# Filling a weight ring only where its expert changes, and asking for rows elsewhere in SyncE's order

## The reference

```python
logits = xn @ router_w                       # 8 experts
topv, topi = jax.lax.top_k(softmax(logits), 2)
topv = topv / sum(topv)
for e in range(8):                           # F = 1024
    gate, up = split(xn @ gate_up_w[e])
    out += comb[:, e] * ((silu(clip(gate, -10, 10)) * up) @ down_w[e])
out += swiglu(xn, shared_gate_up_w, shared_down_w)
```

## Time and profile before

| | |
|---|---|
| median of 3 executions | 1149.23 us (1145.25 to 1150.15) |
| profiled execution, its own time | 1156.33 us |
| its span | 1154.6 us |
| TensorE busy | 1041.0 us (90%) |
| VectorE busy | 800.8 us (69%) |
| DMA, mean | 214 GB/s, 246.72 MB |
| transfers into `single_ring`, issued | 144 in this record, of 768 KB |

### The profile page before, as it was taken

How to read it: one execution, slowest core, us unless ns; L and a number is a source line. 1 busy time by engine, 2 the same in 40 slices (tenths; PEclk the granted TensorE clock), 3 DMA queues, 4 the chain that set the end, 5 groups by cost and what they waited for, 6 DMA issues and landing times.

```text
span 1154.6 us, 22702 instructions
## 1 busy us (share of the span) xinstructions
PE 1041.0 (90%) x7042; PEld 917.3 (79%) x7042; DVE 800.8 (69%) x2051; ACT 623.7 (54%) x1269; POOL 287.1 (25%) x302
## 2 busy tenths in 40 slices
PE   4889999999988998899999999999998699998940
PEld 2666777677666655899999999999998699998940
DVE  5996899897879767566666666666665366665645
ACT  6768868777775364354544544344444244443415
POOL 1133032743252445021212112121121112111125
PEclk9999999999999999899999999999999999999975
DMA  8664766874675588872837264893939945398249
GB/s 305 210 219 168 261 204 223 299 248 146 220 237 188 200 287 300 283 270 65 283 76 235 39 209 128 301 359 76 374 91 330 352 118 164 100 351 263 57 94 216
DMA packets 130715, 246.72 MB, mean 214 GB/s; under 512 B 10848, under 2 KB 76128, under 8 KB 130656
## 3 DMA queue, kind: packets, MB, share of 16 engines
q1 hardware_dynamic: 115248, 226.08, 56.2%
q0 software_dynamic: 15408, 19.93, 9.6%
HBM read 357.61 MB, written 85.50 MB: 384 GB/s over the span
## 4 chain that ended last, share of the span: by engine, by line
PE 68%; DMA 8%; DVE 7%; SPq 7%; issue 4%; ACT 3%; POOL 2%; another core or an unknown queue 1%; DVEq 0%; ACTq 0%; POOLq 0%
PE bank L477 12%; PE bank L1432 8%; PE bank L1434 8%; PE bank L1433 8%; PE bank L1477 4%; PE bank L1479 4%; PE bank L1478 4%; PE bank L471 4%; PE bank L472 4%; PE bank L473 4%; DMA w_both<-w_split 3%; SPq L1302 2%; SPq L1303 1%; PE bank L1448 1%; PE bank L1450 1%
## 5 line engine op out<-in xcount | busy, mean ns | idle before, releaser
L1614 DVE TENSOR_SCALAR cv<-bank 128x256 f32<-128x256 f32 x284 | 120.3, 424 | 182.9 <-PE bank L1434 148.5
L1381 POOL DMA_INDIRECT acc_scratch<-cv,ids x71 | 111.1, 1564 | 541.9 <-DVE cv L1577 518.5
L1544 ACT ACTIVATE cv<-cv 128x256 f32<-128x256 f32 x284 | 118.4, 417 | 210.5 <-DVE cv L1614 207.3
L1432 PE MATMUL bank<-h_hi,w_both 128*128 128x256 f32 x744 | 209.8, 282 | 18.1 <-DMA w_both<-w_split 15.4
L1433 PE MATMUL bank<-h_hi,w_both 128*128 128x256 f32 x744 | 207.3, 279 | 0.0
L1434 PE MATMUL bank<-h_hi,w_both 128*128 128x256 f32 x744 | 207.3, 279 | 0.0
L1432 PEld LDWEIGHTS bank<-h_hi,w_both 128*128 128x128 f32 x744 | 141.0, 190 | 22.0 <-issue 10.5
L1530 ACT ACTIVATE h_lo<-cv 128x256 fp32r<-128x256 f32 x248 | 103.1, 416 | 88.3 <-DVE cv L1617 87.3
L1617 DVE TENSOR_TENSOR cv<-bank,cv 128x256 f32<-128x256 f32 x284 | 120.2, 423 | 41.0 <-ACT cv L1544 37.2
L1434 PEld LDWEIGHTS bank<-h_hi,w_both 128*128 128x128 f32 x744 | 140.9, 189 | 0.0
L1433 PEld LDWEIGHTS bank<-h_hi,w_both 128*128 128x128 f32 x744 | 140.9, 189 | 0.0
(11 more groups left out here) (268 smaller groups left out, 2653.8 us busy)
## 6 DMA issues: line engine op xcount, KB each, us to landing
single_ring<-w_split SPq DMA_DIRECT2D x144, 768.0 KB
w_both<-w_split SPq DMA_DIRECT2D x180, 512.0 KB
w_both<-w_split SPq DMA_DIRECT2D x180, 256.0 KB
e_raw<-w_e SPq DMA_DIRECT2D x64, 384.0 KB
w_split<-e_high SPq DMA_DIRECT2D x64, 384.0 KB
w_split<-e_raw SPq DMA_DIRECT2D x64, 384.0 KB
xs_hi<-w_split SPq DMA_DIRECT2D x30, 512.0 KB
xs_lo<-w_split SPq DMA_DIRECT2D x30, 512.0 KB
```

Source lines behind the costliest of these rows:

```text
L1432: nc.tensor.matmul(out, gu_hi[f][:, cols], xg_hi[:, par, c, :], start=c == 0, stop=False)
L1614: nc.vector.tensor_scalar(half, gate_ps, CLIP, -CLIP, ALU.min, ALU.max).then_inc(clipped, 1)
```

## The change

The second ring is filled only for a single slot whose expert differs from the last single slot's. The plan computes `fresh` for that, multiplies the old flag (`steady`) by it, and writes two tables of nine flags behind each other into `group_change`: fill in the turn n % 4 = 2, and fill in the turn n % 4 = 3. That is five more small VectorE instructions in steps 6 and 7 of slot 0. The ring's eight chunks become three tensors of 5, 2 and 1 places, each filled by one transfer, issued behind chunks 0, 1 and 2. The row request moves from behind chunk 1 to behind chunk 0, and in the turns behind a single slot to behind chunk 7. The rows of slot 2 are asked for ahead of the waits for `ends_cleared` and the scatters.

```diff
-H_AT, XNT_AT, FULL_AT = 146080, 162496, 219456
+H_AT, XNT_AT, FULL_AT = 146336, 162752, 219712
...
+        steady, fresh = [decay[:, 1, (9 + i) * 48:(9 + i) * 48 + NS] for i in range(2)]
+        single_ring = [nc.alloc_sbuf_tensor_at(f"single_ring{at}", [P, places, 2 * CW], F32R, offset=at)
+                       for at, places in ((XNT_AT, 5), (H_AT, 2), (FULL_AT, 1))]
...
             store_shared(2 * B - 1)
+            sp.wait_ge(plan_ready, 1)
+            third_rows()
             sp.wait_ge(ends_cleared, 16 * (E + 2))
             for half in range(2):
                 sp.wait_ge(scattered[half], B * 16 * HT * K)
-            sp.wait_ge(plan_ready, 1)
             other_groups()
...
-            nc.vector.tensor_tensor(group_change[:, NP:SLOTS], thirds[:, :, 2], thirds[:, :, 1], ALU.is_equal)
+            nc.vector.tensor_tensor(steady[:, :], thirds[:, :, 2], thirds[:, :, 1], ALU.is_equal)
...
+                    nc.vector.memset(fresh[:, 0:1], 1.0)
+                    planned(nc.vector.tensor_tensor(fresh[:, 1:NS], code[:, 1:NS], code[:, 0:NS - 1], ALU.not_equal))
...
+                    planned(nc.vector.tensor_tensor(steady[:, :], steady[:, :], fresh[:, :], ALU.mult))
+                    nc.vector.tensor_copy(group_change[:, NP:SLOTS], steady[:, :])
+                    nc.vector.tensor_tensor(group_change[:, SLOTS:SLOTS + NS], fresh[:, :], steady[:, :], ALU.subtract)
...
-        def load_single(f, e, wanted):
-            sp.dma_start(w_single[f][:, :].bitcast(F32), w_s[e, f, :, :], cond=wanted).then_inc(single_loaded, 16)
+        def load_singles(part, e, wanted):
+            first = sum(v.shape[1] for v in w_single[0:part])
+            to = w_single[part].bitcast(F32)
+            sp.dma_start(to, w_s[e, first:first + to.shape[1], :, :].rearrange("f p c -> p f c"), cond=wanted).then_inc(single_loaded, 16)
...
-                flag = to_come if n % BODY == 2 else table_at(i, n - 1)
+                flag = to_come + (0 if n % BODY == 2 else NS)
...
                 load_chunk(f, e, new)
-                if f == 1:
+                if f == (FC - 1 if single(n - 1) else 0):
                     next_rows(i, n)
-                if loads_single:
+                if loads_single and f < len(w_single):
                     if f == 0 and n > BODY:
                         sp.wait_ge(down_done, before(i, n - n % BODY, steps_at) + FC // 2 + FC)
-                    load_single(f, e_single, wanted)
+                    load_singles(f, e_single, wanted)
...
-            next_rows(0, 1)
             free(sp, "x1")
...
-                pe.wait_ge(single_loaded, before(i, n, ones_at) * (32 * FC) + 32 * FC)
+                pe.wait_ge(single_loaded, before(i, n, ones_at) * (32 * len(w_single)) + 32 * len(w_single))
...
-        group_change = sb("group_change", [P, SLOTS], I32)
+        group_change = sb("group_change", [P, SLOTS + NS], I32)
...
+        sb("apart", [P, 3 * LT * 2])
```

More of the change, by code:

```diff
@@ L144, in mixer @@
         unused, expert_f, passed_f, row_f, starred = [decay[:, 1, (4 + i) * 48:(4 + i) * 48 + NP] for i in range(5)]
-        singles_at = [XNT_AT + k * 8 * CW for k in range(5)] + [H_AT + k * 8 * CW for k in range(2)] + [FULL_AT]
-        single_ring = [nc.alloc_sbuf_tensor_at(f"single_ring{f}", [P, 2 * CW], F32R, offset=at) for f, at in enumerate(singles_at)]
+        steady, fresh = [decay[:, 1, (9 + i) * 48:(9 + i) * 48 + NS] for i in range(2)]
+        single_ring = [nc.alloc_sbuf_tensor_at(f"single_ring{at}", [P, places, 2 * CW], F32R, offset=at)
+                       for at, places in ((XNT_AT, 5), (H_AT, 2), (FULL_AT, 1))]
         banks = [ctx.enter_context(nc.psum_tensor(f"bank{i}", [P, HALF], F32)) for i in range(8)]
@@ L230, in mixer @@
         x1 = [by_tile(flat(v[:, :, :])[:, k * TC * D:(k + 1) * TC * D]) for v in (e_raw, e_high) for k in range(2)]
-        homes = (gu_ring, d_ring, single_ring, quad(u_flat[:, R_AT:R_AT + 2 * GT * ROW]), quad(x_home[0]), quad(x_home[1]),
+        homes = (gu_ring, d_ring, [v[:, :, :] for v in single_ring], quad(u_flat[:, R_AT:R_AT + 2 * GT * ROW]), quad(x_home[0]), quad(x_home[1]),
                  u_flat[:, R_AT + 2 * GT * ROW:R_AT + 2 * GT * ROW + DC * G].rearrange("p (c g) -> p c g", g=G),
@@ L360, in _ @@
         def _(sp):
-            rows_of_star, weights_of_star, other_groups = e_sync(sp)
+            rows_of_star, weights_of_star, third_rows, other_groups = e_sync(sp)
             def load_x(b, half):
@@ L1244, in experts @@
     by_chunk = lambda v: v.rearrange("p (m c k) -> p c m k", m=2, c=DC)
-    gus_hi, gus_lo = [[by_chunk(v[:, at:at + 4 * P]) for v in w_single] for at in (0, CW)]
-    ds_hi, ds_lo = [[v[:, at + 4 * P:at + CW] for v in w_single] for at in (0, CW)]
+    places = [v[:, k, :] for v in w_single for k in range(v.shape[1])]
+    gus_hi, gus_lo = [[by_chunk(v[:, at:at + 4 * P]) for v in places] for at in (0, CW)]
+    ds_hi, ds_lo = [[v[:, at + 4 * P:at + CW] for v in places] for at in (0, CW)]
     ids = sb("ids", [P, 2, GT], I32)
@@ L1370, in others @@
             sp.wait_ge(out_added, 16 * (NC // 2))
-        return first_rows, first_weights, others
+        return first_rows, first_weights, lambda: next_rows(0, 1), others
     def gpsimd(pool):
```

## The result

The change makes the kernel faster, by about half of what was forecast. Median of four executions 1135.01 us (1130.57 to 1136.60), against 1149.69 us (1145.25 to 1151.73) for four of the kernel before: a ratio of 0.9871, 95% interval 0.983 to 0.9912, so 14.7 us less. The forecast was 1120.0, with 1110 to 1134 as range. The profiled execution took 1134.12 us; the one of before took 1156.33, so from profile to profile 22.2 us went, and 7.5 of these were not there in the medians.

What follows compares the result with a forecast made beforehand. TensorE, busy 90%, was taken as the bound, its expert-stage waiting nearly all for first-ring weights. Ten slots' 36.6 us excess less 6.3 kept gave 30.3 gained; off the median 1118.9, or 1126.0 if surplus was stall; taken 1120.0, range 1110 to 1134.

Steps and rivals of the forecast that it cites:

- slots 17 and 37: Turns behind a single slot: weight waits (2.81 + 3.78 us) go; the later row request stalls 0 to 2, 0.9 kept each.
- slots 19, 22, 23, 34, 35: Slots losing the fills of turns 18, 22 and 35: of 6.24 us over, 0.7 kept for a second chunk put back.
- slots 26 and 27: Experts 3 and 4 in succession: removing a 6.29 MB fill takes out 15.3 of 17.9 us; 3 kept, bounds 0 and 10.
- slot 1 and the plan: Slot 1, 5.87 us over: 0.4 kept waiting for slot 2's rows, 0.4 for five new VectorE instructions.
- the sentence on the landing: Row request in turns 17 and 37: lands in 2.8 to 5.4 us, rows there between 728.4 and 731.0, wanted at 729.02.
- a rival with a chance of 0.12: Slot 2's rows stay late behind pad stores, 1125; likewise turns 17 and 37 behind weights, 2 us each, 1129 with both; 0.12.
- the three steps that chunks are ahead: Slots 19, 22, 23, 34, 35: chunks' lead, some 6 us of a 16.8 us slot, covers most of the second chunk's delay.
- The first rival: Slot 27 keeps most of a stall because bytes for experts 3 and 4 exceed two slots: 10 us, not 3; 1127; chance 0.12.
- the other reading: The profile's 7.1 us above the median is stall that ordinary runs lack, so the forecast would be 1126.0 instead of 1118.9.
- Nothing or little, as forecast: Fills staying in turns 2, 6, 10: nothing, up to 1 us; new VectorE instructions: 0 to 0.9 us, taken as 0.4.
- The slower rival: Nine turns behind a single slot: request over 2.1 us later stalls each, 5.9 us apiece, 53 in all; 1172; chance 0.03.

Runs made afterwards that it cites:

- the fills alone: Kernel before with only the fills' new flags: eight transfers a fill, only for the three single slots whose expert changes, requests unmoved; 1135.52 us, ratio 0.9872.
- two kernels with the old request: Kernel before with only the fills' flags changed (1135.52 us), and kernel before with only the row request's places moved (1157.16 us); slot 2's rows requested as before.
- the early request alone: Kernel before with only the request for slot 2's rows moved ahead of the waits; 1148.35 us, ratio 0.9986.
- the two runs with the request behind the first transfer: Changed kernel, request behind chunk 1 in ordinary turns; behind a single slot, behind chunk 7 in one (1151.28 us), chunk 5 in the other (1141.41 us).
- the places alone: Kernel before with only the row request moved, behind chunk 0, and chunk 7 behind a single slot; nine fills of eight transfers; 1157.16 us, ratio 1.0084.

## Why the prediction was wrong, and where it was right

The sum was made of what each slot would keep over its undisturbed length. Put beside what they kept in the profile after:

| step of the prediction | over before, us | to be kept | kept | gained less |
|---|---|---|---|---|
| slots 17 and 37 | 6.59 | 1.8 | 9.79 | 8.0 |
| slots 19, 22, 23, 34, 35 | 6.24 | 0.7 | 4.61 | 3.9 |
| slots 26 and 27 | 17.91 | 3 | 2.08 | -0.9 |
| slot 1 and the plan | 5.87 | 0.8 | 0.1 | -0.7 |
| together | 36.6 | 6.3 | 16.6 | 10.3 |

- **Slots 17 and 37: the step that failed.** The prediction had the right wait and the right place: "What is late next is the request itself." Both waits for weights went, as it said. It also had the delay of its issue: 1.5 us forecast, 1.6 measured. What failed is the sentence on the landing, "Such a request takes 2.8 to 5.4 us to land". That bracket came from turns in which the request stands behind chunk 1 of the first ring, 2.8 with the queue run empty and 5.4 with chunks 0 and 1 under way; here eight chunks went ahead, 1.89 and 1.75 MB of them had not moved, and it was 6.7 and 6.5 us. The wait came out at 3.44 and 2.89 us where 0 to 2 were allowed. Then the price: a wait was taken as its own length, and here slots 17 and 37 lost 1.8 and 1.7 us more to the clock. The case itself stood among the rivals ("The same would happen in turns 17 and 37, behind weights, 2 us each"), at half its size, in a rival with a chance of 0.12. The two runs with the request behind chunks 5 and 6 show that what stands ahead on the queue decides. A row that would have warned lay in the trace of before: the row request of turn 27, between weights, took 6.5 us, outside the stretch from which the earlier trace rows was taken.
- **Slots 19 and 23.** The fills' removal did what was forecast for 22, 34 and 35, which keep 0.2 of 2.77. But slot 23 rose from 17.80 to 18.60 as slot 22 fell from 17.84 to 16.81, so the two together gained only 0.2. For 19 and 23 the prediction named the price, a second chunk put back by the request, and covered it with "the three steps that chunks are ahead". That cover was not reached for chunk 1. SyncE's queue of the kernel after, turn 19:

```profile
752.15 0.56 SPq L1311 DMA_DIRECT2D w_both<-w_split  x1
753.72 0.37 SPq L1299 DMA_DIRECT2D u<-xs_scratch  x1
...
754.80 0.56 SPq L1310 DMA_DIRECT2D w_both<-w_split  x1
```

  2.65 us lie between the second transfer of chunk 0 and the first of chunk 1, which goes out at 754.80; between 759 and 761 us TensorE stands and waits for weights, 1.5 us in all, the slot's only wait. In the four kernels with three transfers a fill and the request behind chunk 1 slot 19 took 17.37, 17.87, 17.36 and 18.31 us, in the order in which they stand above; in the three with it behind chunk 0 18.99, 20.84 and 18.58. Slot 23 took 17.79, 18.32, 18.81 and 17.76 against 18.60, 18.57 and 18.32: these overlap, and for slot 23 the cause stays open.
- **Slots 26 and 27** were right in kind and in size: three fills stayed, six went, and all but 2.1 of 17.9 us went. The rate behind it holds too: 399 GB/s with pair weights alone from 714 to 722 us, beside 387. With the fills alone the two slots keep 4.9, so 13.0 of the 15.8 us are the fills' doing. The other 2.8 came with the rest of the change: with the request behind chunk 1 and three transfers a fill the two slots took 17.95 and 17.79 us, 2.3 over, so they are likely not owed to the request's place; which other part brought them was not tried alone. The first rival fell.
- **Slot 1** was right within the profile, at 16.92 us and a clock of 1.00, and wrong for the median. The prediction took 5.5 us of gain from one execution, in which that slot ran at a clock of 0.85, and counted it in full while it spread the profile's surplus of 7.1 us over the whole time. Most of that surplus was this very stall. The prediction saw the other reading ("if those 7.1 us are stall that ordinary runs do not have, 1126.0"), which was the better one: a second execution had 0.8 to gain there, two kernels with the old request 1.8 and 1.6, and the early request alone gains nothing that can be measured. Had it been set aside, the forecast would have stood some 5 us higher.
- **Nothing or little, as forecast:** SyncE's 83.0 us at the request are gone, five more VectorE instructions cost nothing that shows, and the large transfers delay nobody, for the reason given (the row request ahead of them). That reason is a condition, as the two runs with the request behind the first transfer show.
- **The slower rival** did not come in the seven turns in which nothing is loaded, and its price is right in order of size for the two others: 5.2 and 4.6 us a slot, where it said 5.9. On the fills of before, the moved request alone makes the kernel slower, by 0.84%.

So the ten slots gained 20.0 us and not 30.3. Slot 1 also begins 1.2 us earlier (477.95 against 479.17), and 1.0 lies elsewhere: 22.2 from profile to profile. For the medians 7.5 come off: the profiled execution of before lay 6.6 above its median, of which 5.0 are slot 1, and that of after 0.9 below its own. The parts don't add up: the fills alone bring 13 us, the moved request alone costs 8.7, and both with the rest bring 14.7. With the fills gone the moved request costs less, since slots 17 and 37 go from 20.17 and 22.59 to 22.65 and 21.96, 1.8 us more together, where with all fills there they go from 20.20 and 22.56 (the second profile of before) to 22.95 and 25.65, 5.8 more.

## What to carry to other kernels

A small transfer that the next step needs pays for every byte that stands ahead of it on its queue and has not moved, so moving it past big transfers must be priced by these bytes, and not by its latency in the quiet. Look for the place where it is neither so early that it blocks the queue on its own wait nor so late that the queue is full: here two chunks earlier won 8 us. And before a stall at one place is counted as gain, see whether a second execution has it.

## What was not expected of the hardware

- How steep the cost is: the same request landed in 2.8 us in the quiet, in 3.9 with 0.82 MB still ahead of it, in 6.7 with 1.76 to 1.89, and in 8.7 in turn 37 of the kernel with the places alone, where a fill of the second ring had gone out just ahead of the first ring's.
- An idle TensorE did not always cost clock. 3.44 us of waiting took 5.2 us in slot 17 of the kernel after (granted 0.92 over the slot). 1.76 us took 2.0 in slot 17 behind chunk 6 (1.00). 1.92 us took 4.25 in slot 19 behind chunk 5 (0.92), while in the kernel after the same slot waited 1.55 us and kept a clock of 1.00. So nearly the same wait cost clock in one place and not in another; why, these runs don't settle.
- The first microseconds of a first-ring fill move fewer bytes than its middle. In the kernel after, turn 19:

```profile
755.00:757.00 2.00, 2.00 (x20) 2.00 (x20) 1.52 (x4) 0.90 (x3) 0.30 (x1) 1.00 1.23 234
757.00:759.00 2.00, 2.00 (x20) 2.00 (x19) 1.18 (x3) 0.84 (x2) 0.00 (x0) 1.00 0.98 266
759.00:761.00 2.00, 0.73 (x7) 0.54 (x5) 1.18 (x3) 0.83 (x2) 0.00 (x0) 1.00 1.06 330
```

  The DMA engines' share is full from the start, and the bytes are 234 to 330 GB/s, against 399 in the middle of turn 17's fill. It was not tried what takes the rest.
